# Later weight casts in the norm stage, slots placed one shared block sooner, and halves of the last blocks' rows made sooner

## Time and profile before

| | us |
|---|---|
| median of three runs | 1311.24 (1308.58 to 1312.24) |
| the profiled execution | 1311.47 |
| its span in the trace | 1309.6 |
| TensorE busy (matmul) | 1221.8 |
| ScalarE busy | 995.9 |
| VectorE busy | 976.1 |
| GpSimd busy | 567.7 |

### The profile page before, as it was taken

The page is one execution under the profiler, slowest core; times in us unless marked ns, Lnnn a source line. Parts: engine busy times, 40 slices in busy tenths (PEclk is TensorE's granted clock), DMA queues, the critical chain, the costliest instruction groups (busy, mean ns, idle before and its releaser), DMA issues.

```text
span 1309.6 us, 29563 instructions
## 1 busy us (share of the span) xinstructions
PE 1221.8 (93%) x9377; PEld 936.7 (72%) x9440; DVE 976.1 (75%) x1945; ACT 995.9 (76%) x2039; POOL 567.7 (43%) x574
## 2 busy tenths in 40 slices
PE   3799999999999999868999979999999999999896
PEld 2444444444444444337899969999999999999896
DVE  5788887888788888628666647877777777777578
ACT  4599998999899999846744437777787777777677
POOL 5332322232223220006446654666666666666553
PEclk8799999999999999988799989999999999999998
DMA  9300101010000000432013237777777777776354
GB/s 298 111 18 3 34 2 36 2 34 2 20 2 18 2 18 18 140 115 89 18 54 110 85 104 242 241 240 238 239 251 249 249 243 246 238 240 219 109 186 160
DMA packets 125412, 161.25 MB, mean 123 GB/s; under 512 B 17088, under 2 KB 108224, under 8 KB 125312
## 3 DMA queue, kind: packets, MB, share of 16 engines
q1 hardware_dynamic: 118496, 141.25, 33.2%
q0 software_dynamic: 6816, 18.75, 4.0%
HBM read 122.06 MB, written 37.52 MB: 122 GB/s over the span
## 4 chain that ended last, share of the span: by engine, by line
PE 77%; DMA 9%; DVE 6%; ACT 3%; issue 2%; POOL 2%; SPq 0%; ACTq 0%; another core or an unknown queue 0%; DVEq 0%; POOLq 0%
PE att_psV L387 9%; PE att_psA L330 9%; PE att_psB L340 8%; DMA slots_x<-sent_rows,all_slot 6%; PE exp_psU L1587 5%; PE exp_psU L1589 5%; PE exp_psU L1588 5%; PE exp_psD L1572 5%; PE exp_psD L1573 5%; PE exp_psD L1574 5%; PE att_psT L354 4%; PE att_psX L408 2%; PE att_psX L410 2%; PE att_psX L409 2%; PE exp_psT L1560 1%
## 5 line engine op out<-in xcount | busy, mean ns | idle before, releaser
L529 DVE TENSOR_REDUCE att_mx<-att_psA 128x1 f32<-128x512 f32 x512 | 338.0, 683 | 74.2 <-PE att_psA L330 73.2
L445 ACT ACTIVATE att_prob<-att_psB 128x512 f32<-128x512 f32 x512 | 299.2, 599 | 53.0 <-PE att_psB L340 39.3
L1632 ACT ACTIVATE exp_psU<-exp_psU,ew_b 128x256 f32<-128x256 f32 x312 | 126.9, 446 | 103.2 <-PE exp_psU L1589 103.2
L330 PE MATMUL att_psA<-att_qk 96*128 96x512 bf16 x512 | 196.7, 386 | 6.2 <-DVE att_mx L529 2.4
L340 PE MATMUL att_psB<-att_qk 128*128 128x512 bf16 x449 | 172.6, 386 | 14.1 <-issue 5.4
L1683 DVE CAST exp_hh<-exp_psU 128x512 fp32r<-128x512 f32 x156 | 107.9, 692 | 101.6 <-ACT exp_psU L1632 101.6
L1572 PE MATMUL exp_psD<-exp_w2h,exp_hh 128*128 128x256 f32 x624 | 175.8, 282 | 0.0
L1587 PE MATMUL exp_psU<-exp_xh,exp_w1h 128*128 128x256 f32 x624 | 173.6, 278 | 1.4 <-DVE exp_xl L1674 1.4
L1589 PE MATMUL exp_psU<-exp_xh,exp_w1l 128*128 128x256 f32 x624 | 173.2, 278 | 0.0
L1588 PE MATMUL exp_psU<-exp_xl,exp_w1h 128*128 128x256 f32 x624 | 173.2, 278 | 0.0
L1573 PE MATMUL exp_psD<-exp_w2l,exp_hh 128*128 128x256 f32 x624 | 172.5, 276 | 0.0
(11 more groups left out here) (206 smaller groups left out, 3228.7 us busy)
## 6 DMA issues: line engine op xcount, KB each, us to landing
ew_w<-ew SPq DMA_DIRECT2D x40, 1024.0 KB, 5.6
exp_w<-ew SPq DMA_DIRECT2D x38, 1024.0 KB, 5.8
slots_x<-pre_acc SPq DMA_DIRECT2D x13, 780.0 KB, 10.3
pre_spare<-slots_x SPq DMA_DIRECT2D x39, 260.0 KB, 4.6
out_g<-rows_y SPq DMA_DIRECT2D x32, 256.0 KB, 3.2
ew_b<-eb SPq DMA_DIRECT2D x39, 128.0 KB
pre_spare<-xT SPq DMA_DIRECT2D x8, 512.0 KB, 4.5
attn_rows<-att_ob SPq DMA_DIRECT2D x8, 512.0 KB, 2.8
```

The lines of the kernel that those rows point to most:

```text
L330: pe.matmul(psA[A_BANK[n % U]][:, :], r[:, 0, qt * P:(qt + 1) * P], r[:, 1, :], start=True, stop=True).then_inc(s_amm, 1)
L445: act.activation(prob[:, n % PR, :], psB[B_BANK[n % U]][:, :], ACT.Exp, scale=SCALE).then_inc(s_exp, 1)
L529: dve.reduce_max(mx[:, g % 2, n % U:n % U + 1], psA[A_BANK[n % U]][:, :], AX_X).then_inc(s_max, 1)
```

## The change

Four edits; attention is the same.

- `SPLIT_FROM` goes from 6 to 10: the eight casts on ACT sit in slots 10, 12, ..., 24 where they sat in slots 6, 8, ..., 20, and POOL's eight follow tiles 5, 7, ..., 19 where they followed 1, 3, ..., 15.
- `RANK_AFTER` goes from 1 to 0: the four rank matmuls stand after `up` of block 0, and DVE's `place()` stands ahead of `rows_lo(2)` and `add(0)`.
- In the combine stage POOL makes the hidden lo halves of block 0 too, and DVE none; DVE's `rows_lo(2)` follows pair 1 where it followed pair 0.
- ACT's `rows_hi(n+1)` stands at the head of slot 4n, ahead of the relus, where it stood at the end of slot 4n+1.

```diff
@@ norm_and_route
-    SPLIT_FROM = 6
+    SPLIT_FROM = 10
@@ shared_and_dispatch
-    RANK_AFTER = 1
+    RANK_AFTER = 0
@@ shared_and_dispatch, vector
             shared.rows_lo(dve, Nth(1))
+            place()
             shared.rows_lo(dve, Nth(2))
             shared.add(dve, Nth(0))
-            place()
@@ combine, gpsimd
-            for n in range(1, NB):
-                if n == 1:
-                    pool.wait_ge(shared.lo_ready, shared.HC)
+            for n in range(NB):
                 for h in range(shared.HC):
                     shared.hidden_lo(pool, Nth(n), h)
@@ combine, vector
             shared.rows_lo(dve, Nth(0))
-            for h in range(shared.HC):
-                shared.hidden_lo(dve, Nth(0), h)
             rows_ahead(1)
...
-                if k == 0:
+                if k == 1:
                     rows_ahead(2)
@@ combine, scalar
                 n, h = divmod(2 * slot, shared.HC)
+                if h == 0 and n + 1 < NB:
+                    shared.rows_hi(act, Nth(n + 1))
                 if slot < SLOTS:
                     shared.relu(act, Nth(n), h)
                     shared.relu(act, Nth(n), h + 1)
-                if h == 2 and n + 1 < NB:
-                    shared.rows_hi(act, Nth(n + 1))
```

## The result

The changed kernel takes **1298.3 us** (median of 6 runs, 1297.58 to 1303.5) against 1310.6 us before, timed beside it. The ratio is 0.9918, 95% interval 0.9896 to 0.9939. Two repeats beside other kernels gave 0.9923 (0.9901 to 0.9946) and 0.9925 (0.9901 to 0.9949). The medians lie 12.3 us apart in this pair and 9.2 and 8.5 in the repeats; by the ratios, which use all runs, it is 10.7, 10.1 and 9.8. So the change is worth some 10 us, where 13.9 were forecast; the forecast time was 1297.4 us, in a range of 1293.5 to 1302.5.

What follows compares the result with a forecast made beforehand. PE was taken to decide most of the time, idling at three places around the edits; gains of 3.2 + 6.3 + 4.4 = 13.9 us gave 1297.4 us against the median, range 1293.5 to 1302.5.

Steps and rivals of the forecast that it cites:

- Which places bound the kernel: PE idles in norm slot 6, before the experts at the end of dispatch, and between up(0) and up(1) in combine.
- Weight casts, 3.2 us: Norm stage: ACT's 7.07 us wait goes, DVE waits for residual block 2 instead; 3.2 us gained, ends 0 and 4.3.
- the 0.5 us charged for low clock and casts together: Norm stage: allowance for slow first slots and casts, taking the 3.7 us gain at block 2 to 3.2.
- late next: Norm stage: residual block 2's load, behind 2 MB of weights until 593.0, becomes what DVE waits for.
- Slots, 6.3 us: Dispatch: first scatter 6.35 us sooner, chain length kept, experts' row load earlier; 6.3 us gained, ends 3.0 and 8.5.
- The tie that was forecast: End of dispatch: last scatter lands near 775.3, last `add` ends near 775.1, 0.7 us sooner; the limit passes to PE.
- Combine, 4.4 us: Combine: 2.63 us PE idle before up(1) and 1.63 us low clock go; 4.4 us taken, ends 1.5 and 4.7.
- rival (A): One of the three parts gives little, 3 to 6 us lost: 1300.5 to 1303.5, say 1302 us; chance 0.17.
- (B): PE's clock stays up at the shorter norm and pre-experts pauses, giving 0.8 and 2.2 us: 1294.4 us; chance 0.17.
- (C): Dispatch scatters started sooner take longer, making the kernel slower: 1316 to 1334 us; chance 0.04.
- (D): A hidden second wait keeps the experts' first row load at 781.66, only 7.6 us gained: 1303.7 us; chance 0.03.
- the forecast's own signs: Wrong if mean scatter step exceeds 1.6 us, ACT waits for POOL's combine half, or any gain is below half.

Runs made afterwards that it cites:

- the kernel without casts: Changed kernel with SPLIT_FROM back at 6 (slots and combine changed, casts as before): 1348.15 us, ratio 0.9973 to the kernel before.
- the casts alone: Kernel before with only the eight weight casts later (SPLIT_FROM 10): ratio 1.0002 (0.9988 to 1.0017).
- The kernel with block 2 first: Changed kernel with shared weight loads behind residual block 2's load and SPLIT_FROM 12: 1294.3 us, ratio 0.9874 to the kernel before.
- the slots alone: Kernel before with only ranks and place() one block sooner (RANK_AFTER 0, place() ahead of rows_lo(2)): 4.2 us gained.
- second group: Experiments run on another chip, including four scatter semaphores against two; the kernel before took 1350.9 us there (22 runs).
- combine alone: Kernel before with only the combine-stage edits: 3.4 us gained.
- the order: Kernel before with only the combine order changed, block 0's hidden halves staying on DVE behind rows_ahead(1), rows_hi early: 1306.0 us, ratio 0.9968.
- the engine: Kernel before with only block 0's hidden halves of the combine stage given to POOL: 1306.1 us, ratio 0.9969.

## Why the prediction was right or wrong

**Which places bound the kernel:** right for all three; each wait named is gone where the forecast put it.

**Weight casts, 3.2 us:** the wait moved as forecast, and the size was wrong. What to count from matters here. The first residual addition comes 2.30 us behind PE's first instruction of the stage in the kernel before and in all five traces with late casts, but 2.75 to 3.25 us behind it in the other six with old casts, whose PE runs its first projections at low clock in part or whole. First projection of the kernel before, then of the kernel without casts:

```profile
577.28 1.10 PE L829 MATMUL nrm_psP<-pre_spare,nrm_aT 128*128 128x256 f32 x4 [0.41 <-ACT nrm_aT L863]
```
```profile
576.92 2.04 PE L829 MATMUL nrm_psP<-pre_spare,nrm_aT 128*128 128x256 f32 x4 [0.41 <-ACT nrm_aT L863]
```

This is made up for by the addition that needs block 1. So the terms below count from PE's first instruction of the stage (576.21 before).

The addition that needs block 2 starts there at 16.6 to 17.3 us with late casts (mean 17.1, five traces) and at 19.3 to 20.5 with old ones (mean 20.0, seven traces): 2.95 us sooner, where the forecast read 3.7. Of the missing 0.7, 0.4 are the profiled kernel before, at 20.46 the highest of the seven, and 0.3 the landing, forecast at 16.8. Behind it 1.1 us are lost up to the last addition (41.7 against 40.6 us on average) and 0.6 behind that, up to the first `up`. This leaves 1.2 us of 3.2; the times of the casts alone, which give nothing or at most 1.6, agree. The term that was mis-sized is thus the 0.5 us charged for low clock and casts together: 1.8 us went there. Most of the 1.1 is low clock: the one trace with late casts whose clock stayed full took 40.95 us over this stretch, the four where it fell 41.7 to 42.6. The kernel with block 2 first, full clock as well, took 40.2. The 0.6 goes with the granted clock at the end of the stage, 0.60 to 0.64 in three of the five traces and 0.76 and 0.77 in the other two, which took 1.6 us less there; that the casts set this isn't shown. The forecast saw the load of block 2 as "late next" and stopped there. Removing the wait is what pays: 4.8 us of the norm stage, and 6.7 in the times.

**Slots, 6.3 us:** the first scatter came 6.47 us sooner (6.35 forecast), straight behind POOL's fills: right. In the profiled pair the last landing set the row load before and after (132.41 and 124.79 us behind the first `up`), so the load's 7.6 us are the 6.5 of the start, 0.7 of a shorter chain of starts and 0.5 of a quicker last landing, which the forecast had kept the same. The mis-sized term is the last `add`, 0.7 us forecast and 2.5 measured; with 0.7 it would have ended at 126.0 and held the load there. PE's wait at `down` of block 2 was counted from one window as 0.66 and 0.1 us; but the gaps from start to start of its matmuls there, 0.94 in place of 0.113 us and then 0.2 to 0.3 more at each pair, sum to some 2.1 us, because DVE made that block's halves just in time for a while longer. They are gone in the trace of the change and of the slots alone. The tie that was forecast came: the `add` is 0.6 and 1.0 us ahead of the last landing in these two traces, and in the other three of kernels with the new slots (second group aside) it is the `add` that is late, by 2.0 to 5.6 us. This is where the gain shrinks to the 4.2 us of the times (last section).

**Combine, 4.4 us:** 4.7 in the profiled pair, 3.4, 4.0 and 4.0 us in the times of combine alone, of the order and of the engine. The 2.63 us of idle always go. The 1.63 us of low clock go only where the old kernel had it: with the old order two traces at the same pace took 72.9 us (idle 2.71, clock 0.59 in the 4 us behind it) and 70.8 us (idle 2.24, clock 1.00). With the new order that pace gives 68.2, so the edit is worth 4.7 us in the one case and 2.6 in the other, and the times of 3.4 to 4.0 lie between. That DVE reaches `add(3)` on PE's heels was right, 0.45 us of waiting; that POOL's half wouldn't hold ACT too. That both edits were needed for it was not asked, and they aren't.

**Sum:** 13.9 forecast, 14.9 in the three stages of the profiled pair, some 10 in the times. The measured median, 1298.3 us, is 0.9 from the forecast time, and that closeness is luck: four of the six times lie at 1297.6 to 1298.5 and two at 1303.4, and the repeats spread over 1296 to 1305. By the ratios 3 to 4 us of the 13.9 didn't come. That is what rival (A) had, with the casts as the part that gives little. (B) was true in the norm stage in one of five traces with the late casts and false at the experts' start in the profiled one. (C) did not come: the mean step stayed at 98.49 / 63 = 1.56 us. (D) fell. By the forecast's own signs a gain below half of its term was wrong, and the casts' is.

## What to carry to other kernels

Where a wait is removed by moving its consumer, look at what the queue behind the producer holds: putting the small urgent transfer ahead of the large patient one gained some 7 us, where moving the consumer alone had gained nothing that could be measured. Take a difference of two starts in one execution as one draw, and count it from a point that the clock doesn't move: from the first residual addition the gain at block 2 came out as 2.3 us over these traces, from PE's first instruction of the stage as 2.95. When two engines can each hold the next stage, look in every trace which came last before giving a gain to either. When an engine's lateness is priced, count its gaps from start to start until it runs at full pace again, not only the idle time ahead of the first instruction.

## What the runs showed of the hardware that was not expected

**Two paces of PE at full clock.** Windows of PE, two in the shared stage and one in combine, granted clock 1.00 in all; the first trace of the change, then its third:

```profile
690.00:700.00 10.00, 10.00 (x91) 1.00 0.21 74
740.00:750.00 10.00, 10.00 (x91) 1.00 0.26 93
1260.00:1270.00 10.00, 10.00 (x87) 1.00 0.70 206
```
```profile
690.00:700.00 10.00, 10.00 (x87) 1.00 0.25 84
740.00:750.00 10.00, 10.00 (x87) 1.00 0.27 95
1260.00:1270.00 10.00, 10.00 (x91) 1.00 0.58 177
```

The same matmuls start every 0.1133 us or every 0.1178 us, through a whole stage, and a stage can have the one and another stage the other in the same execution. In the shared stage the slow pace puts the end of the last `add` 128.3 to 128.4 us behind the first `up` with the new slots, in place of 124.2 and 124.3; with the old ones it is 129.6 (one trace) in place of 125.8 to 126.7. With the old slots the scatters' lateness hides it (dispatch 137.0 to 137.9 us at the fast pace, 136.1 in the one trace at the slow one); with the new slots most of it is paid (130.2 and 130.9 against 133.3 to 133.9). So the slots gain about 6.7 us at the one pace and, by that one trace, 2.5 at the other, and the times of the slots alone, 4.2, lie between. The change's own two groups of times fit this: the profiled execution of 1298.2 us had the fast pace in the shared stage, those of 1303.1 and 1302.8 the slow one. In combine the two paces give 68.1 to 68.2 and 69.7 to 69.8 us with PE never idle. What sets the pace is open.

**The clock behind a short pause is not settled by the pause's length.** In the norm stage it stayed full behind 1.18 us and was low behind 1.66, 1.78, 2.08 and 2.20; in combine it stayed full behind 2.24 and was low behind 2.63, 2.71 and 2.72. Within each stage the longer pauses were the ones that cost the clock, but 2.24 us in one left it full where 1.66 in the other didn't.

**A group in which the other engines stood still while scatters ran.** In the second group, on its own chip, the kernel before took 1350.9 us for 1310, and every kernel profiled there lost some 40 us or more in the shared stage while scatters ran, as told above. Whether the chip or something else in that group made it, and its cause, are open.
